# Context products in five matmuls instead of six, with the second tile of the 192 columns split across its two halves

## The reference

```python
# layer 0: routing and a gated update
tok = ctx @ W_proj + b_proj                      # 120x192 @ 192x256 in each batch
attn = softmax(x @ tok.T / sqrt(256))
routed = attn @ tok
...                                              # layernorms, gates r, u, n, 256 wide
# layer 1: three phases, each over the 8 batches
x = attention(h, h,   Wq, Wk, Wv, Wo, bo) + x    # self, 16 heads of 64
x = attention(h, ctx, Wq, Wk, Wv, Wo, bo) + x    # cross: k = ctx @ Wk, v = ctx @ Wv, both 192x1024
x = (u * gelu(gate)) @ ff_Wo + ff_bo + x
```

## Time and profile before

| | |
|---|---|
| median of 3 runs | 1088.36 us (1087.58 to 1089.52) |
| the profiled execution's own time | 1088.15 us |
| its span, first to last instruction | 1086.4 us |
| TensorE busy | 92% of the span, 7872 matmuls |
| VectorE, ScalarE, GpSimd busy | 65%, 58%, 33% |
| mean granted TensorE clock | 0.969 |

### The profile page before, as it was taken

The page is one execution under the profiler, slowest core; times in us unless marked ns, Lnnn a source line. Parts: engine busy times, 40 slices in busy tenths (PEclk is TensorE's granted clock), DMA queues, the critical chain, the costliest instruction groups (busy, mean ns, idle before and its releaser), DMA issues.

```text
span 1086.4 us, 21327 instructions
## 1 busy us (share of the span) xinstructions
PE 997.5 (92%) x7872; PEld 937.3 (86%) x7872; DVE 710.9 (65%) x1598; ACT 626.5 (58%) x1945; POOL 357.2 (33%) x474
## 2 busy tenths in 40 slices
PE   5688874599999999999999999999999998899998
PEld 4577753489999999899999899999999997899998
DVE  4466744596766676667667775666677667566664
ACT  3466452386656575657566765666666666533333
POOL 1101324033334333333333244454554454401010
PEclk9999887699999999999999998999999999999999
DMA  6221000100200000000000300300000001010100
GB/s 205 68 68 39 20 20 20 44 11 2 98 2 21 1 21 1 21 1 21 2 21 3 101 25 1 103 25 2 25 26 18 8 21 46 17 38 21 40 30 21
DMA packets 28121, 34.62 MB, mean 32 GB/s; under 512 B 2164, under 2 KB 21364, under 8 KB 28020
## 3 DMA queue, kind: packets, MB, share of 16 engines
q1 hardware_dynamic: 28020, 33.26, 9.9%
HBM read 24.86 MB, written 8.39 MB: 31 GB/s over the span
## 4 chain that ended last, share of the span: by engine, by line
PE 79%; DVE 10%; ACT 6%; issue 2%; POOL 1%; DMA 1%; SPq 1%; DVEq 0%; POOLq 0%
PE bank L1306 17%; PE bank L1307 16%; PE bank L1308 16%; PE bank L1523 8%; PE bank L1506 5%; PE bank L1564 3%; PE bank L1565 3%; PE bank L1566 3%; PE bank L1538 3%; ACT p L721 1%; PE bank L1480 1%; PE bank L1414 1%; DVE bn L887 1%; PE bank L1415 1%; PE bank L1416 1%
## 5 line engine op out<-in xcount | busy, mean ns | idle before, releaser
L721 ACT ACTIVATE p<-bank,negmax 128x256 f32<-128x256 f32 (+1 forms) x512 | 208.2, 428 | 18.0 <-DVE negmax L1088 15.1
L538 POOL TENSOR_TENSOR oT_hi<-oT,ones 128x256 fp32r<-128x256 f32 x128 | 94.0, 735 | 378.0 <-DVE oT L1111 378.0
L731 ACT CAST pT_hi<-bank 128x512 fp32r<-128x512 f32 (+1 forms) x256 | 110.7, 485 | 166.1 <-PE bank L1523 165.3
L1306 PE MATMUL bank<-hT_hi,w_hi 128*128 128x256 f32 x640 | 190.6, 298 | 5.9 <-DVE hT_lo L1072 2.5
L1308 PE MATMUL bank<-hT_hi,w_lo 128*128 128x256 f32 x640 | 181.5, 284 | 0.0
L1307 PE MATMUL bank<-hT_lo,w_hi 128*128 128x256 f32 x640 | 181.3, 283 | 0.0
L1306 PEld LDWEIGHTS bank<-hT_hi,w_hi 128*128 128x128 f32 x640 | 122.6, 192 | 9.2 <-DVE hT_lo L1072 4.8
L1103 DVE TENSOR_TENSOR pT_lo<-bank,pT_hi 128x512 fp32r<-128x512 f32 (+1 forms) x256 | 129.7, 548 | 0.3
L1084 DVE TENSOR_REDUCE negmax<-bank 128x2 f32<-128x512 f32 x128 | 82.2, 684 | 66.8 <-PE bank L1506 66.8
L1307 PEld LDWEIGHTS bank<-hT_lo,w_hi 128*128 128x128 f32 x640 | 122.9, 192 | 0.0
L1308 PEld LDWEIGHTS bank<-hT_hi,w_lo 128*128 128x128 f32 x640 | 122.6, 192 | 0.0
(11 more groups left out here) (200 smaller groups left out, 2787.2 us busy)
## 6 DMA issues: line engine op xcount, KB each, us to landing
w_stage<-in_weights SPq DMA_DIRECT2D x52, 256.0 KB, 4.8
x_in<-x_dram SPq DMA_DIRECT2D x24, 256.0 KB, 2.9
x_dram<-x_out SPq DMA_DIRECT2D x16, 256.0 KB, 3.2
l_x<-in_x SPq DMA_DIRECT2D x4, 512.0 KB, 5.6
x_dram<-l_out SPq DMA_DIRECT2D x4, 512.0 KB, 2.9
out_dram<-x_out SPq DMA_DIRECT2D x8, 256.0 KB, 3.1
l_ctx<-in_ctx SPq DMA_DIRECT2D x4, 240.0 KB, 5.3
ctx_in<-in_ctx SPq DMA_DIRECT2D x8, 120.0 KB, 3.2
```

The lines of the kernel that those rows point to most:

```text
L538: nc.gpsimd.tensor_tensor(oh[:, G % PAIRS, :], of[:, :], ones[:, :], ALU.mult).then_inc(y["o_hi"], 1)
L721: last = nc.scalar.activation(p[:, G % 2, e, t * cols:(t + 1) * cols], scores_at(G, e, t), ACT.Exp, bias=negmax[:, G % 2, t, e:e + 1], acc ...
L731: nc.scalar.copy(pTh[0:r, G % 2, e, 0:n], bank[4 + e][0:r, 0:n]).then_inc(y["pT_hi"], 1)
L1306: nc.tensor.matmul(dst, lh, rh, start=(i == 0), stop=False)
```

## The change

The zeros in the second tile are replaced. Rows 64 to 127 of the second tile of the transposed context now hold the low part of the same 64 context columns whose high part stands in rows 0 to 63, and the second tile of the weights holds its 64 real rows twice. One matmul over 128 rows then gives high by high and low by high together, and the remaining one, low weights by high context, reads rows 0 to 63 only. Five matmuls make up a product instead of six.

```diff
+RC = DC - 128
...
+            def context_product(dst, w, x, weights_stay):
+
+                (wh0, wl0), (wh1, wl1), (xh0, xl0, x1) = *w, x
+                pairs = ((wh0, xh0), (wh0, xl0), (wl0, xh0), (wh1, x1), (wl1[0:RC, :], x1[0:RC, :]))
+                for i, (a, c) in enumerate(pairs):
+                    last = nc.tensor.matmul(dst, *((a, c) if weights_stay else (c, a)), start=(i == 0), stop=(i == 4))
+                return last
...
                 for g in range(4):
-                    last = product(k_bank(b, c)[:, g * SC:(g + 1) * SC],
-                                   [(wcols(A2W + "k", kt, (4 * c + g) * 128, 128), (ch[:, kt, :], cl[:, kt, :]))
-                                    for kt in range(KT)])
+                    last = context_product(k_bank(b, c)[:, g * SC:(g + 1) * SC],
+                                           [wcols(A2W + "k", kt, (4 * c + g) * 128, 128) for kt in range(KT)],
+                                           (ch[:, 0, :], cl[:, :], ch[:, 1, :]), True)
...
             def context_low(b):
                 dve.wait_ge(y["cT_hi"], b - B + 1)
-                nc.vector.tensor_tensor(cl[:, :, :], c_src(), ch[:, :, :].bitcast(F32),
-                                        ALU.subtract).then_inc(y["cT_lo"], 1)
+                nc.vector.tensor_tensor(cl[:, :], c_src()[:, 0, :], ch[:, 0, :].bitcast(F32), ALU.subtract)
+                nc.vector.tensor_tensor(ch[RC:2 * RC, 1, :], c_src()[RC:2 * RC, 1, :],
+                                        ch[RC:2 * RC, 1, :].bitcast(F32), ALU.subtract).then_inc(y["cT_lo"], 1)
...
-                sp.dma_start(cin[:, :], ctx_p[bass.ds(b - B, 1), :, :].rearrange("b s d -> (b s) d")
-                             ).then_inc(y["c_in"], 16)
+                csrc = ctx_p[bass.ds(b - B, 1), :, :].rearrange("b s d -> (b s) d")
+                sp.dma_start(cin[:, 0:DC], csrc[:, 0:DC]).then_inc(y["c_in"], 16)
+                sp.dma_start(cin[:, DC:D], csrc[:, 128:DC]).then_inc(y["c_in"], 16)
...
-                for i, (c, col) in enumerate(UNITS[n].src):
-                    sp.dma_start(stage[:, n % STAGES, i, :], weights[c][:, col:col + HALF]).then_inc(staged[n % STAGES], 16)
+                for c, col, width, at, twice in UNITS[n].src:
+                    dst, src, done = stage[:, n % STAGES, at:at + width], weights[c][:, col:col + width], staged[n % STAGES]
+                    if twice:
+                        sp.dma_start(dst[0:RC, :], src[0:RC, :]).then_inc(done, 16)
+                        sp.dma_start(dst[RC:2 * RC, :], src[0:RC, :]).then_inc(done, 16)
+                    else:
+                        sp.dma_start(dst, src).then_inc(done, 16)
```

More of the change, by code:

```diff
@@ L59 @@
       "L1_xattn_ff_Wp": 4096, "L1_xattn_ff_Wo": 0}
+A1W, A2W = "L1_xattn_a1_W", "L1_xattn_a2_W"
 Unit = namedtuple("Unit", "src at width half scaled")
@@ L72, in columns, with staged_until @@
     c = sum(WCHUNKS[:phase]) + 2 * WSETS[phase].index(name)
-    return Unit(((c, half * HALF), (c + 1, half * HALF)), AT[name], 2 * CH, half, name.endswith("Wq"))
-A1W, A2W = "L1_xattn_a1_W", "L1_xattn_a2_W"
-UNITS = [whole(0, c, c * CH) for c in range(4)] \
+    twice = name in (A2W + "k", A2W + "v")
+    return Unit(((c, half * HALF, HALF, 0, False), (c + 1, half * HALF, HALF, HALF, twice)),
+                AT[name], 2 * CH, half, name.endswith("Wq"))
+def staged_until(n):
+    return sum(16 * sum(1 + twice for *_, twice in UNITS[m].src) for m in range(n % STAGES, n + 1, STAGES))
+FIRST = Unit(((0, 0, D, 0, False), (0, D, D, D, True), (0, 2 * D, HALF, HALF, False)), 0, CH, 0, False)
+UNITS = [FIRST] + [whole(0, c, c * CH) for c in range(1, 4)] \
     + [columns(A1W + "q", 0), columns(A1W + "k", 0), columns(A1W + "q", 1), columns(A1W + "k", 1)] \
@@ L173, in build @@
             cTh = sb("l0_cT_hi", [128, KT, L0B * SC], F32R, where=l0)
-            cTl = sb("l0_cT_lo", [128, KT, L0B * SC], F32R, where=l0)
+            cTl = sb("l0_cT_lo", [128, L0B * SC], F32R, where=l0)
             tTh = sb("l0_tokT_hi", [128, KT, L0B * SC], F32R, where=l0)
@@ L229, in build @@
                 ch = sb("cT_hi", [128, KT, SC], F32R, where=att)
-                cl = sb("cT_lo", [128, KT, SC], F32R, where=att)
+                cl = sb("cT_lo", [128, SC], F32R, where=att)
             kdh = qkh[:, :, 1, 0:2 * SC]
@@ L284, in weights_hi @@
         def weights_hi(act, n):
-            act.wait_ge(staged[n % STAGES], 32 * (n // STAGES + 1))
-            src, dst = stage[:, n % STAGES, :, :], unit_of(WH, n)
+            act.wait_ge(staged[n % STAGES], staged_until(n))
+            src, dst = stage[:, n % STAGES, :].rearrange("p (a n) -> p a n", a=2), unit_of(WH, n)
             if UNITS[n].scaled:
@@ L913, in lo_context @@
                 dve.wait_ge(z["cT_hi"], it + 1)
-                nc.vector.tensor_tensor(cTl[:, :, :], first_c(), cTh[:, :, :].bitcast(F32),
-                                        ALU.subtract).then_inc(z["cT_split"], 1)
+                nc.vector.tensor_tensor(cTl[:, :], first_c()[:, 0, :], cTh[:, 0, :].bitcast(F32), ALU.subtract)
+                nc.vector.tensor_tensor(cTh[RC:2 * RC, 1, :], first_c()[RC:2 * RC, 1, :],
+                                        cTh[RC:2 * RC, 1, :].bitcast(F32), ALU.subtract).then_inc(z["cT_split"], 1)
             def lo_tokensT(it):
@@ L1335, in first_tokensT @@
                 for m in range(KT):
-                    last = product(bank[4][:, m * 256:m * 256 + L0B * SC],
-                                   [(wcols("L0_xattn_W_proj", kt, m * 128, 128), (cTh[:, kt, :], cTl[:, kt, :]))
-                                    for kt in range(KT)])
+                    last = context_product(bank[4][:, m * 256:m * 256 + L0B * SC],
+                                           [wcols("L0_xattn_W_proj", kt, m * 128, 128) for kt in range(KT)],
+                                           (cTh[:, 0, :], cTl[:, :], cTh[:, 1, :]), True)
                 last.then_inc(z["tokT"], 1)
@@ L1344, in first_tokens @@
                     cc = slice(c * SC, (c + 1) * SC)
-                    last = product(bank[4][0:SC, c * D:(c + 1) * D],
-                                   [((cTh[:, kt, cc], cTl[:, kt, cc]), wcols("L0_xattn_W_proj", kt, 0, D))
-                                    for kt in range(KT)])
+                    last = context_product(bank[4][0:SC, c * D:(c + 1) * D],
+                                           [wcols("L0_xattn_W_proj", kt, 0, D) for kt in range(KT)],
+                                           (cTh[:, 0, cc], cTl[:, cc], cTh[:, 1, cc]), False)
                 last.then_inc(z["tok"], 1)
@@ L1484, in context @@
             def context(b):
-                pe.wait_ge(y["c_in"], 16 * (b - B + 1))
+                pe.wait_ge(y["c_in"], 32 * (b - B + 1))
                 for kt in range(KT):
@@ L1602, in project_values @@
                         pe.wait_ge(w_ready, (13, 18)[c])
[L1603 to L1606, removed]
+                w = [wcols((A1W if b < B else A2W) + "v", kt, c % 2 * 512, 512) for kt in range(KT)]
+                dst = v_bank(b, c)[0:v_rows(b), :]
+                if b < B:
+                    last = product(dst, list(zip(left, w)))
+                else:
+                    last = context_product(dst, w, (ch[:, 0, :], cl[:, :], ch[:, 1, :]), False)
+                last.then_inc(y["v"], 1)
             def project_keys(b, c):
```

14 lines of the change are left out of this document (7 added, 7 removed).

## The result

The changed kernel takes 1111.39 us (median of 6 runs, 1109.04 to 1112.97), the kernel before 1088.72 us (6 runs, 1087.40 to 1089.92). The ratio is 1.0206 with a 95% interval of 1.0189 to 1.0222: 2.1% slower. The forecast was 1113.5 us in 1106 to 1119. The profiled execution of the changed kernel took 1112.42 us, with a span of 1110.6 us and a mean granted clock of 0.956 (0.969 before). So the total came out, and in part by luck: of its terms, the keys were 6.4 us too large and the clock 6 us too small, and the two nearly cancelled.

A forecast was written before the change was run, and what follows sets the result against it. The prediction took TensorE as the bound; keys 17.9, slow-clock keys 1.1, values 1.3, layer 0 3.4, start 1.0 and VectorE 0.4 made 25.1 us on 1088.15 us, and with 0.2 us for the median 1113.5 us, range 1106 to 1119.

The forecast's parts named there:

- What bounds the kernel: Whole kernel: TensorE, busy 92% of the span and 79% of the chain, so its added work counts nearly in full.
- Keys, "+0.28 us" a product, 17.9 us: Cross phase: each of 64 products of keys goes from 0.66 to 0.94 us, +17.9 us in all.
- I take the full 0.39 and not a part: Every product: going to 64 rows and back charged at 0.39 us, as read in the self phase.
- only the two gaps: Rival, every product: a row change costs 0.18 us, not 0.39, as weights load in time; 1095 us, chance 0.10.
- Four of these products run just after the 2.02 us wait: First cross-phase batch: four products of keys at granted clock 0.50 pay twice the extra, 1.1 us more.
- the clock falls as well: Rival, cross phase: 3.4 us at the lower clock after each of 16 calls, 27 us more, 1140 us; chance 0.04.
- the prediction's own last sentence: Sign of being wrong: a product of keys at 0.73 us or less, or cross-phase clock falls in more places than one.
- Values, 1.3 us for the 8 on the path, nothing for the 8 ahead of the wait: Cross phase: 8 products of values at +0.16 us each make +1.3 us; the 8 at i = 3 are covered.
- Layer 0, 3.4 us: Layer 0: six products on the chain cost +0.57 us each at the lower clock level; the other ten are covered.
- Start, +1.0 us: Start: extra transfer issues delay the first weight unit's landing and copy by 0.5 to 1.4 us, taken as +1.0.
- VectorE, +0.4 us: VectorE: `cT_lo` as two instructions costs +0.13 us, on TensorE's path twice in layer 0 and once before layer 1.
- costs nothing: Rival, every product: a row change is free for one tile, so the kernel is faster, 1079.5 us; chance 0.04.

The follow-up runs named there:

- probe_of_widths: Kernel before, with matmuls of 512, 256, 120 and 60 columns, plain and with row changes, added after the last output between 512-column ones; 1142.13 us with the added work.
- full_rows: Changed kernel, with the fifth matmul of each product reading all 128 rows instead of 64; 1081.84 us, ratio 0.9937.
- keys_64_rows_last: Changed kernel, with the four 64-row matmuls of each call of keys together at its end; 1091.10 us, ratio 1.0024.
- start_in_pieces: Kernel before, with the first weight unit in four transfers instead of two and each layer 0 context load in two instead of one; 1090.18 us, ratio 1.0016.

## Why the prediction was right, and where it was not

**What bounds the kernel.** Right. TensorE's added time counted nearly in full, the self phase and the feed-forward kept their length, and the wait for `oT` stayed, at 0.77 for 0.88 us.

**Keys, "+0.28 us" a product, 17.9 us.** The mechanism was right, the size was not, and the step is the one that the prediction put as "I take the full 0.39 and not a part". It was read between matmuls of 256 and 512 columns; keys stream 120. There the round trip is 0.28 us, as probe_of_widths shows for 120 columns by itself, and the product 0.84 us, +0.17 or 0.18 us. The 64 products cost about 11.5 us. The bound given for this step (0.05 us less in coming back) went in the right direction. The 0.28 us lie halfway between the 0.39 of the forecast and the 0.18 of the rival "only the two gaps".

**"Four of these products run just after the 2.02 us wait", 1.1 us, and the rival "the clock falls as well".** This is the term that was far too small: the falls cost some 7.2 us. The prediction gave the rival a chance of 0.04 and 27 us, with a fall behind each of 16 calls; it came in part, with 20 us more at 0.50 in the cross phase and only behind some of the calls. The argument against it was that the self phase changes rows too and keeps the full spacing. But there it is paid once in 12 matmuls of 256 columns, here in every fifth of 120. The other argument, that the low stretch of the kernel before follows its wait of 2.02 us, does not hold either: in probe_of_widths the same first batch has the same wait, no fall behind it, and takes 37.76 us instead of 42.54. By the prediction's own last sentence, which counted falls in more places than one as a sign of being wrong, this step was. Both full_rows and keys_64_rows_last show that the falls go when the round trips do. The estimate of twice the price at the lower level was too high as well: a round trip with 120 columns is 0.37 us there and 0.28 at the full clock. And the first batch, for which the 1.1 us were put, grew by 1.2 us (44.89 against 43.67), less than an undisturbed one, as its low stretch is 6.8 us long and not 10.2.

**Values, 1.3 us for the 8 on the path, nothing for the 8 ahead of the wait.** Right: 0.05 us longer in the product and 0.10 in the next matmul, 0.15 us for a predicted 0.16. Those at i = 3 shortened the wait from 0.88 to 0.77. So the undisturbed batch is 8 x 0.18 + 0.15 = 1.6 us longer by the single rows and 1.54 by its length, not 2.40.

**Layer 0, 3.4 us.** The timeline of PE at the last `first_tokens`, at a granted clock of 0.50, the first two and the last two matmuls of the second product and what follows:

```profile
128.65 0.57 PE L1336 MATMUL bank<-w_hi,l_cT_hi 128*120 128x256 f32 x1
129.01 0.41 PE L1336 MATMUL bank<-w_hi,l_cT_lo 128*120 128x256 f32 x1
...
129.44 0.41 PE L1336 MATMUL bank<-w_hi,l_cT_hi 128*120 128x256 f32 x1
129.79 0.57 PE L1336 MATMUL bank<-w_lo,l_cT_hi 64*120 64x256 f32 x1
130.28 0.79 PE L1440 MATMUL bank<-l_inT_hi,w_hi 128*128 128x512 f32 x1
```

The product takes 1.63 us against 6 x 0.213 = 1.28: +0.35, where "2 x 0.39 - 0.21" gave +0.57, because neither part of the price doubles: into the 64-row matmul 0.35 us, out of it 0.49, and 0.36 for the one behind, 0.14 + 0.28 + 0.15 = 0.57 us over the plain 0.21 and not 0.78. Six of them are 2.1 us and not 3.4. **Start, +1.0 us:** 1.3 us in the profile of start_in_pieces, 0.3 to 3.2 us by its medians. **VectorE, +0.4 us:** the two instructions take 0.266 + 0.285 us against 0.39, +0.16 for a predicted +0.13, three times 0.5 us. Together these make 3.9 of the 4.7 us. What the other 0.8 us are is open: either some of the ten products counted as covered, or the clock, which up to the transposes at 200.46 was low for 50 us against 43 before, in stretches that lie elsewhere in each execution. full_rows, which has no change of rows there, still stands 2.1 us late at the same place, with 44 us.

**The sum.** By single rows 11.5 (keys) + 1.2 (values) + 7.2 (clock) + 4.7 (layer 0 and start) = 24.6 us against 24.2 measured in the profiles and 25.1 predicted. That the forecast agrees to 1 us rests on the two errors that cancel, and is luck. The rivals "only the two gaps" (1095 us) and "costs nothing" (1079.5 us) fell: the gaps are there and so is, with 120 columns, half of the load. The Trainium skill's sentence in TensorE: Matmul & The Clock Gate, "Why this matters for your kernels", that a single matmul with an inner dimension of 32 takes the same time as one of 128, is borne out for 64 rows inside a row of 64-row matmuls (four in keys_64_rows_last cost one round trip) and not between 128-row ones (0.84 us for the five of a product, 0.56 in full_rows). Its page TensorEngine Tiling, "Key Properties", states that a change of the tiling mode drains TensorE. The 0.09 us gaps agree with it; of the uncovered load beside them it does not speak.

## What to carry to other kernels

Between matmuls of 128 rows, a single one of 64 costs a round trip of 0.28 us with 120 columns and 0.39 with 256, more than the 0.11 to 0.23 us of the matmul that it may have saved; fill the tile to 128 rows (with zeros, or with a term that only adds exactness), or issue all the 64-row ones of a group together. Price such a step from a row with the same number of streaming columns as yours: a price read from wide matmuls was too high for narrow ones here. And where TensorE's stream gets such gaps often, allow for the clock: it took some 7 us here, nearly a third of the loss, though TensorE counts as busy throughout.

## What was unexpected of the hardware

- The granted clock fell to its lower level (1.2 of 2.4 GHz) in stretches in which the profile shows TensorE busy for 100%. That share doesn't show the gaps: the records of the keys last 0.27 to 0.32 us and start 0.11 to 0.25 us apart, so they overlap across them. The one wait of a batch, 0.77 us for `oT`, doesn't explain the falls: full_rows waits there for 1.11 us, and its clock stays up from 659 to 911. In probe_of_widths the same shows with nothing else running. The timeline of PE has eight 512-column matmuls behind the plain 120-column ones, and eight behind those with changes of rows:

```profile
1112.80 2.06 PE L1764 MATMUL bank<-w_lo,w_hi 128*128 128x512 f32 x8
...
1118.78 3.25 PE L1764 MATMUL bank<-w_lo,w_hi 128*128 128x512 f32 x8
```

  2.06 us is their plain length; in the 3.25 us the clock is down from 1119.4 on. After the group of 60 columns it is 2.95 us; after those of 256 and 512 nothing fell, with a granted clock of 1.00 up to 1112. So it fell after changes of rows among narrow matmuls, and not after the same changes among wide ones. The plain narrow ones, after which it did not fall, ran for 1.3 us, the groups with changes for 3.8 to 4.1; longer plain stretches are not tested here, beyond the calls of 2.3 us in full_rows. Why the clock falls, these runs don't show.
- The same instructions can meet a different clock in another execution. The first batch of the cross phase, unchanged in probe_of_widths, waits for `oT` as in the earlier trace rows and then has the full clock, where the profile of the kernel before has 10.2 us at 0.50 (timeline of PE, and the windows view):

```profile
645.26 0.41 PE L1538 MATMUL bank<-ident,rsum_wide 128*128 128x128 f32 x2 [2.02 <-DVE oT L1111]
```

```profile
645.00:683.00 38.00, 36.88 (x306) 35.95 (x307) 27.01 (x68) 25.77 (x101) 18.37 (x27) 1.00 0.04 12
```

- At the lower clock the plain interval doubles (0.111 to 0.213 us with 120 columns), and the price of a change of rows does not: a round trip goes from 0.28 to 0.37 us with 120 columns and from 0.39 to 0.59 with 256.
- Finer loads in layer 0 (four small transfers in place of two for the first weights, two in place of one for the context) made a kernel of 1088 us longer by 0.3 to 3.2 us, which nothing later gave back.
